# Chunk states of a linear scan: six steps in a row replaced by three doublings with powers of the transition matrix

## The reference, cut to what matters

```python
def step(hc, u_t):
    hc = jnp.einsum('bdr,drs->bds', hc, A) + u_t[:, :, None] * Bv[None]
    y = jnp.einsum('bds,ds->bd', hc, Cv)
    return (hc, y)
_, ys = jax.lax.scan(step, h0, u.transpose(1, 0, 2))
y = ys.transpose(1, 0, 2)
return y @ Wout + b_out + res
```

## Time and profile before

| | us |
|---|---|
| median of three runs | 1939.16 |
| lowest and highest run | 1934.07, 1939.63 |
| the profiled execution | 1942.1 |
| its span in the trace | 1940.4 |
| busy in the span: TensorE matmul / weight load | 1724.4 / 1318.3 |
| busy in the span: DVE / ACT / POOL | 1185.5 / 979.3 / 852.3 |

### The profile page before, as it was taken

The page is one execution under the profiler, slowest core; times in us unless marked ns, Lnnn a source line. Parts: engine busy times, 40 slices in busy tenths (PEclk is TensorE's granted clock), DMA queues, the critical chain, the costliest instruction groups (busy, mean ns, idle before and its releaser), DMA issues.

```text
span 1940.4 us, 25449 instructions
## 1 busy us (share of the span) xinstructions
PE 1724.4 (89%) x8004; PEld 1318.3 (68%) x8004; DVE 1185.5 (61%) x2758; ACT 979.3 (50%) x1906; POOL 852.3 (44%) x866
## 2 busy tenths in 40 slices
PE   6989998779999899999999888889899888888799
PEld 6979997757767677776767655656665555555565
DVE  5542215767677777767686825444356666677765
ACT  3612001656556656565656667666545444445442
POOL 3841201335555545454545453444457666651100
PEclk9989558789999999999999989898899888889999
DMA  6001001087332323233223452221001101002233
GB/s 85 1 2 24 1 1 33 17 198 180 107 93 91 98 85 98 88 98 93 93 88 118 122 149 66 66 86 42 28 12 33 29 23 23 23 31 74 81 109 93
DMA packets 131183, 134.92 MB, mean 70 GB/s; under 512 B 56614, under 2 KB 75306, under 8 KB 131050
## 3 DMA queue, kind: packets, MB, share of 16 engines
q1 hardware_dynamic: 120904, 132.35, 24.5%
q10 hardware_dynamic: 10146, 0.94, 0.6%
HBM read 127.93 MB, written 5.31 MB: 69 GB/s over the span
## 4 chain that ended last, share of the span: by engine, by line
PE 39%; DVE 18%; ACT 12%; issue 7%; POOL 4%; DMA 2%; SPq 1%; DVEq 0%; ACTq 0%; POOLq 0%
PE ypsum L1156 7%; PE flow_G L100 4%; PE flow_G L102 3%; PE flow_G L101 3%; DVE flow_a L1701 2%; DVE flow_a L1707 2%; PE flow_U L100 2%; DVE flow_phi L1485 2%; PE flow_U L101 2%; PE flow_U L102 2%; POOL flow_alo L1790 2%; ACT flow_ahi L1186 1%; ACT xn_tokens L1218 1%; PE flow_side L100 1%; DVE flow_at_rneg L1673 1%
## 5 line engine op out<-in xcount | busy, mean ns | idle before, releaser
L1790 POOL TENSOR_TENSOR flow_alo<-flow_a,flow_ahi 128x512 fp32r<-128x512 f32 x264 | 341.6, 1294 | 339.8 <-ACT flow_ahi L1186 339.3
L100 PE MATMUL flow_G<-xn_hi,flow_hi 128*128 128x512 f32 x520 | 283.9, 546 | 37.6 <-DVE flow_a L1701 22.4
L1701 DVE TENSOR_TENSOR flow_a<-flow_G,flow_mask 128x512 f32<-128x512 f32 x256 | 175.7, 686 | 160.8 <-ACT flow_G L1360 135.4
L1360 ACT ACTIVATE flow_G<-flow_G 128x512 f32<-128x512 f32 x256 | 149.0, 582 | 141.1 <-PE flow_G L102 140.5
L101 PE MATMUL flow_G<-xn_lo,flow_hi 128*128 128x512 f32 x520 | 212.6, 409 | 0.0
L102 PE MATMUL flow_G<-xn_hi,flow_lo 128*128 128x512 f32 x520 | 212.1, 408 | 0.0
L1707 DVE TENSOR_TENSOR flow_a<-flow_U,flow_a 128x512 f32<-128x512 f32 x296 | 204.7, 691 | 9.9
L1186 ACT ACTIVATE flow_ahi<-flow_a 128x512 fp32r<-128x512 f32 x264 | 165.4, 627 | 86.6 <-DVE flow_a L1707 85.5
L1799 POOL TENSOR_TENSOR flow_b<-flow_b,flow_mask 128x512 f32<-128x512 f32 x96 | 126.8, 1327 | 148.5 <-ACT flow_b L1364 77.7
L1799 POOL TENSOR_TENSOR flow_a<-flow_a,flow_mask 128x512 f32<-128x512 f32 x96 | 127.8, 1342 | 105.8 <-ACT flow_a L1364 54.4
L100 PEld LDWEIGHTS flow_G<-xn_hi,flow_hi 128*128 128x128 f32 x520 | 102.2, 197 | 103.9 <-issue 42.2
(11 more groups left out here) (535 smaller groups left out, 3936.3 us busy)
## 6 DMA issues: line engine op xcount, KB each, us to landing
flow_mask<-mask_rows_top SPq DMA_DIRECT2D x512, 128.0 KB, 3.0
flow_mask<-mask_rows_top SPq DMA_DIRECT2D x64, 256.0 KB, 3.2
flow_mask<-mask_rows_zone SPq DMA_DIRECT2D x64, 256.0 KB, 3.2
flow_mask<-mask_rows_steps SPq DMA_DIRECT2D x32, 256.0 KB, 4.0
x<-in_L_attn_x SPq DMA_DIRECT2D x8, 256.0 KB, 5.9
flow_raw<-in_L_ffn_expert_gate_k SPq DMA_DIRECT2D x16, 128.0 KB, 3.6
flow_raw<-in_L_ffn_expert_up_k SPq DMA_DIRECT2D x16, 128.0 KB, 3.6
flow_raw<-in_L_ffn_expert_down_k SPq DMA_DIRECT2D x16, 128.0 KB, 3.9
```

Source lines behind the costliest of these rows:

```text
L100: pe.matmul(out, w_hi, x_hi, start=start, stop=False)
L1360: act.activation(gate, gate, ACT.Silu).then_inc(ev["r_done"], 1)
L1701: dve.tensor_tensor(out, G[at % 2].psum[:, :], weight, ALU.mult).then_inc(ev["t_done"], 1)
L1790: pool.tensor_tensor(alo[i][:, :], acts[i][:, :], ahi[i][:, :].bitcast(F32), ALU.subtract)\
```

## The change

The chunk states are carried by doubling. With P32 the 32nd power that is at hand, and h the states:

1. `one_chunk(i)`: 32 matmuls (4 in each of 8 rounds) with P32, 96 columns (chunks 1 to 6 of 16 sequences); DVE adds the result to chunks 2 to 7.
2. `turned_power(i)`: 32 transposes of P32 into the tile `power`, copied by ACT. `squared(i)`: 32 matmuls with 128 columns, of `power` and P32, give the 64th power, transposed as a stationary operand needs it; ACT copies it to `square`.
3. `two_chunks(i)`: 32 matmuls with the 64th power, 80 columns (chunks 1 to 5); DVE adds to chunks 3 to 7.
4. `four_chunks("half", i)` and `four_chunks("four", i)`: the 128th power as the 64th twice, 2 x 32 matmuls with 48 columns (chunks 1 to 3), 8 in a round; between the two ACT copies to the tile `middle`; behind the second DVE adds to chunks 5 to 7.

`power`, `square` and `middle` lie in `early`, where the pieces of `T0` lie that the near rounds have used. The order on TensorE becomes: 16 near rounds, with a `turned_power` or a `one_chunk` behind each in turn; then `squared` and `two_chunks` in turn, the second two behind the first; then four rounds `half` and four rounds `four`; then the far rounds as before. The 40 state rounds use the same ring of four banks; each waits until the round four before it is evicted, and for what it reads. Far rounds wait for the `four` round of their packs.

```diff
+        self.Hn = self.AT[:, :, :].rearrange("p g m -> p (g m)")[:, 0:PACKS * P].rearrange("p (q n) -> p q n", n=CHUNKS)
+        self.power, self.square = (early[:, 4096 * i:4096 * (i + 1)].rearrange("p (g m) -> p g m", m=P) for i in range(2))
+        self.middle = early[:, 0:PACKS * 48].rearrange("p (g m) -> p g m", m=48)
...
+        def begin(kind, i):
+            n = rounds.number[kind, i]
+            if n >= 4:
+                rounds.wait_evicted(pe, ev, n - 4)
+            return (bank[3], bank[4], bank[5], k.turn)[n % 4]
+
+        def chunk_states(p, first, after):
+            return s.H[:, p, :].rearrange("p (b n) -> p b n", n=CHUNKS)[:, :, first:after]
+
+        def turned_power(i):
+            out = begin("power", i)
+            for q in range(4):
+                last = pe.transpose(out[:, q * P:(q + 1) * P], A[:, 4 * i + q, 0:P], k.ident[:, :])
+            last.then_inc(ev["state_psum"], 1)
+
+        def one_chunk(i):
+            out = begin("one", i)
+            for q in range(4):
+                last = pe.matmul(out[:, q * 96:(q + 1) * 96], A[:, 4 * i + q, 0:P], chunk_states(4 * i + q, 1, 7), start=True, stop=True)
+            last.then_inc(ev["state_psum"], 1)
+
+        def squared(i):
+            rounds.wait_evicted(pe, ev, rounds.number["power", i])
+            out = begin("square", i)
+            for q in range(4):
+                last = pe.matmul(out[:, q * P:(q + 1) * P], s.power[:, 4 * i + q, :], A[:, 4 * i + q, 0:P], start=True, stop=True)
+            last.then_inc(ev["state_psum"], 1)
+
+        def two_chunks(i):
+            rounds.wait_evicted(pe, ev, rounds.number["square", i])
+            rounds.wait_evicted(pe, ev, rounds.number["one", i])
+            out = begin("two", i)
+            for q in range(4):
+                last = pe.matmul(out[:, q * 80:(q + 1) * 80], s.square[:, 4 * i + q, :], chunk_states(4 * i + q, 1, 6), start=True, stop=True)
+            last.then_inc(ev["state_psum"], 1)
+
+        def four_chunks(kind, i):
+            if kind == "half":
+                rounds.wait_evicted(pe, ev, rounds.number["two", 2 * i + 1])
+            else:
+                rounds.wait_evicted(pe, ev, rounds.number["half", i])
+            out = begin(kind, i)
+            for q in range(8):
+                p = 8 * i + q
+                x = chunk_states(p, 1, 4) if kind == "half" else s.middle[:, p, :]
+                last = pe.matmul(out[:, q * 48:(q + 1) * 48], s.square[:, p, :], x, start=True, stop=True)
+            last.then_inc(ev["state_psum"], 1)
...
         def far(r):
             if r == 0:
                 pe.wait_ge(ev["h_zero"], 1)
-                pe.wait_ge(ev["sc_done"], SUBS * (CHUNKS - 2))
                 pe.wait_ge(ev["y_near"], 16)
+            if r % 4 == 0:
+                rounds.wait_evicted(pe, ev, rounds.number["four", r // 4])
...
-        done = 0
-        for n in range(1, CHUNKS - 1):
-            for sub in range(SUBS):
-                if n > 1:
-                    pe.wait_ge(ev["sc_done"], SUBS * (n - 2) + sub + 1)
-                out = (bank[3], bank[4], bank[5], k.turn)[sub]
-                for i in range(8):
-                    p = 8 * sub + i
-                    last = pe.matmul(out[:, i * BATCH:(i + 1) * BATCH], A[:, p, 0:P], s.H[:, p, n:P:CHUNKS],
-                                     start=True, stop=True)
-                last.then_inc(ev["sc_psum"], 1)
-                if (SUBS * (n - 1) + sub) * 16 // 24 >= done:
-                    near(done)
-                    done += 1
-        assert done == 16
+        for r in range(16):
+            near(r)
+            (one_chunk if r % 2 else turned_power)(r // 2)
+        for i in range(10):
+            if i < 8:
+                squared(i)
+            if i >= 2:
+                two_chunks(i - 2)
+        for i in range(4):
+            four_chunks("half", i)
+        for i in range(4):
+            four_chunks("four", i)
         for r in range(16):
             far(r)
```

On ACT a copy of a `power` bank (128x512) stands behind every second near copy, then follow the 8 copies of `square` and the 4 of `middle` (128x384). On DVE the 24 adds (L2434) become 20:

```diff
-        for n in range(1, CHUNKS - 1):
-            for sub in range(SUBS):
-                dve.wait_ge(ev["sc_psum"], SUBS * (n - 1) + sub + 1)
...
+        for kind, i in rounds.order:
+            if kind in rounds.scalar:
+                continue
+            n = rounds.number[kind, i]
+            dve.wait_ge(ev["state_psum"], n + 1)
+            out = (bank[3], bank[4], bank[5], k.turn)[n % 4]
+            first, packs = {"one": (2, 4), "two": (3, 4), "four": (5, 8)}[kind]
+            width = CHUNKS - first
+            h = s.Hn[:, packs * BATCH * i:packs * BATCH * (i + 1), first:CHUNKS]
+            dve.tensor_tensor(h, h, out[:, 0:packs * BATCH * width].rearrange("p (q n) -> p q n", n=width), ALU.add)\
+               .then_inc(ev["state_dve"], 1)
+            if f < PAIRS:
...
```

More of the change, by code:

```diff
@@ L1956, in __init__ @@
                          "shifted stats aggr pool scale_done h_done turned hi lo win_link win_done first bias_done u_psum u_done "
-                         "e_dve e_pool g_turned g_copied ut_turned u2_done v_psum v_done h_zero sc_psum sc_done f_done "
+                         "e_dve e_pool g_turned g_copied ut_turned u2_done v_psum v_done h_zero state_psum state_act state_dve f_done "
                          "t0_in t0_done near_psum y_near y_psum y_done yt_turned yc_act yc_dve", st)
@@ L2199, in near @@
             last.then_inc(ev["near_psum"], 1)
+        rounds = StateRounds()
+        def begin(kind, i):
[39 more added lines that the diff above has]
+            last.then_inc(ev["state_psum"], 1)
         def far(r):
@@ L2241, in _, with __init__, wait_evicted @@
             last.then_inc(ev["yt_turned"], 1)
+class StateRounds:
+    def __init__(self):
+        order = [("one" if r % 2 else "power", r // 2) for r in range(16)]
+        for i in range(10):
+            order += [("square", i)] * (i < 8) + [("two", i - 2)] * (i >= 2)
+        order += [("half", i) for i in range(4)] + [("four", i) for i in range(4)]
+        self.order = order
+        self.number = {key: n for n, key in enumerate(order)}
+        self.scalar = ("power", "square", "half")
+        self.count, n = {}, {"state_act": 0, "state_dve": 0}
+        for key in order:
+            name = "state_act" if key[0] in self.scalar else "state_dve"
+            n[name] += 1
+            self.count[key] = (name, n[name])
+    def wait_evicted(self, pe, ev, n):
+        name, value = self.count[self.order[n]]
+        pe.wait_ge(ev[name], value)
 def finish_y(s, eng, copy, name, parity):
@@ L2313, in _, with state_copy @@
                 .then_inc(ev["u2_done"], 1)
+        rounds = StateRounds()
+        def state_copy(kind, i):
+            n = rounds.number[kind, i]
+            out = (bank[3], bank[4], bank[5], k.turn)[n % 4]
+            act.wait_ge(ev["state_psum"], n + 1)
+            if kind == "half":
+                copy(s.middle[:, 8 * i:8 * i + 8, :], out[:, 0:384].rearrange("p (g m) -> p g m", m=48)).then_inc(ev["state_act"], 1)
+            else:
+                copy((s.power if kind == "power" else s.square)[:, 4 * i:4 * i + 4, :],
+                     out[:, :].rearrange("p (g m) -> p g m", m=P)).then_inc(ev["state_act"], 1)
         for r in range(16):
@@ L2319, in _ @@
                  (bank[0], bank[1], bank[2], k.ypsum)[r % 4][:, :]).then_inc(ev["y_near"], 1)
+            if r % 2 == 0:
+                state_copy("power", r // 2)
+        for i in range(8):
+            state_copy("square", i)
+        for i in range(4):
+            state_copy("half", i)
         finish_y(s, act, copy, "yc_act", 0)
@@ L2428, in _ @@
         dve.wait_ge(ev["v_done"], 8)
-        for n in range(1, CHUNKS - 1):
-            for sub in range(SUBS):
-                dve.wait_ge(ev["sc_psum"], SUBS * (n - 1) + sub + 1)
[L2432 to L2441, removed]
+        rounds = StateRounds()
+        for kind, i in rounds.order:
+            if kind in rounds.scalar:
+                continue
+            n = rounds.number[kind, i]
+            dve.wait_ge(ev["state_psum"], n + 1)
+            out = (bank[3], bank[4], bank[5], k.turn)[n % 4]
+            first, packs = {"one": (2, 4), "two": (3, 4), "four": (5, 8)}[kind]
[4 more added lines that the diff above has]
+            if f < PAIRS:
+                dve.tensor_tensor(s.F[:, 2 * f:2 * f + 2, :, :],
+                                  A[:, 2 * f:2 * f + 2, P:P + CHUNK].unsqueeze(2).to_broadcast([P, 2, PACK, CHUNK]),
+                                  s.mask8[:, :].unsqueeze(1).unsqueeze(3).to_broadcast([P, 2, PACK, CHUNK]), ALU.mult)\
+                   .then_inc(ev["f_done"], 1)
+                f += 1
         for r in range(16):
```

## The result

The changed kernel took 1892.44 us in the median of 4 runs (1891.74 to 1895.07), the kernel before 1939.39 us in 4 runs on the same chip: 46.95 us less, ratio 0.9758 with a 95% interval of 0.9735 to 0.9782. A second set of runs, later, gave 1892.55 against 1941.42 us, ratio 0.9745 (0.9726 to 0.9765). The forecast was 1893.5 us.

A forecast was written before the change was run, and what follows sets the result against it. TensorE bounds the kernel, paying per record for weight loads at a halved clock in the chunk states. 24.1 + 13.8 + 23.8 = 61.7 us against 107.4 saves 45.7: 1893.5 us from the median 1939.16, range 1879 to 1910.

The forecast's parts named there:

- first part: Near rounds, power transposes and `one` rounds: 224 records of 96 to 128 columns at 0.1075 us, 24.1 us.
- second part: `squared` and `two` rounds: 128 records of 128 and 80 columns at 0.1075 us, clock expected to stay, 13.8 us.
- third part: `half` and `four`: 128 records of 48 columns, clock falling 3.4 us after the start, 23.8 us (bounds 13.8 and 27.2).
- stage: Chunk states, from first near or state matmul to first far matmul: 107.4 us before, forecast 61.7 us.
- far rounds: Matmuls after the chunk states: forecast to start at the low clock as before and cost the same 16.4 us.
- saved in the stage: Chunk-state time removed minus time added: 45.7 us, forecast to come off the whole kernel.
- The step with no row behind it: In `half` and `four`: a stream of 48 columns alone, seen in no row, was taken to lose the clock after 3.4 us.
- The waits: In the chunk states: TensorE's waits for ACT, DVE and POOL all hidden; without cover in `squared`/`two`, at most 2 us.
- kept throughout: Rival, chance 0.16: full clock through `half`, `four` and the far matmuls, 58.3 us saved, 1880.9 us.
- Clock lost from the second part on: Rival, chance 0.12: the 80 columns of `two` lose the clock, 32.3 us saved, 1906.9 us.
- the change gives no clock back: Rival, chance 0.08: something other than columns keeps the chunk states' clock low, 8.8 us saved, 1930.4 us.
- The slower rival: Rival, chance 0.03: all 40 state rounds wait for the eviction just ahead, at low clock; 31.2 us slower, 1970 us.

The follow-up runs named there:

- Experiment 1: Kernel before, its six steps and 512 records kept, each state matmul moving 64 columns instead of 16, of which DVE takes 16: 1887.51 us, ratio 0.9717.
- Experiment 3: Changed kernel, order kept, every matmul of one, squared, two, half and four cut to 16 columns, other columns left out: 1911.36 us, ratio 0.9845.
- experiment 4: Changed kernel with 64 columns instead of 48 in the matmuls of half and four: 1884.09 us, ratio 0.9700; in a second set 1878.07 us, ratio 0.9686.
- experiment 5: Changed kernel, every state round waiting for the eviction of the round just ahead instead of four ahead: 1928.02 us, ratio 0.9925 to the kernel before.
- experiments 1 and 2: The second of these: kernel before, 16-column state matmuls reading neighbouring columns of H instead of every eighth, states thus wrong: 1942.11 us, ratio 1.0007.

## Why the prediction was right

**The reading of the bottleneck.** It said that TensorE never waited for DVE in the chain of steps, that a record pays for its weight load and not its columns, and that the granted clock was the larger lever. Experiment 1 bears out the first, the third and half of the second: same records, same chain, four times the columns, 58.3 us. Experiment 3 adds that at full clock narrower matmuls are no cheaper. That it is the weight load which a record pays for stays argued: it fits that TensorE's weight loads fill the stage (106.3 of 107.4 us), but no run made the weight load smaller.

**The terms of the sum.**

| term | forecast, us | measured, us |
|---|---|---|
| first part, 224 records | 24.1 | 25.0 |
| second part, 128 records | 13.8 | 14.3 |
| third part, 128 records | 23.8 | 23.0 |
| stage | 61.7 | 62.3 |
| far rounds | 16.4 | 16.6 |
| saved in the stage | 45.7 | 45.1 |

The price of a record was low, by a misread view. The 93 and 447 records of the earlier trace rows do not all start in their stretch; the view counts each record that lies in it even partly, and at 1.00 a record lasts about 0.27 us while the next start follows after 0.11. The order of time in the same stretch has 24 records in 2.64 us, 0.110 each:

```profile
178.73 1.94 PE L2175 MATMUL ssm_bank<-ssm_turned,ssm_mix 128*128 128x112 f32 x16
180.50 0.60 PE L2163 MATMUL ssm_bank<-ident,ssm_early 128*128 128x128 f32 x4
180.94 0.60 PE L2163 MATMUL turn<-ident,ssm_early 128*128 128x128 f32 x4
181.37 1.94 PE L2175 MATMUL ssm_bank<-ssm_turned,ssm_mix 128*128 128x112 f32 x16
```

Measured are 25.01 us for 224 records, 0.1116 us each, which makes the first two parts 1.4 us longer than forecast. The third part came out 0.8 us shorter, because the clock went 4.6 us into it instead of the 3.4 us taken over from before. With the right prices the forecast's own path would have given about 63.6 us for the stage (an estimate: 352 records at 0.1116, then 30 in 3.4 us, then 98 at 0.213), so a part of the agreement of 61.7 with 62.3 is two errors that cancel.

The step with no row behind it, that 48 columns alone lose the clock, came out as taken, and experiment 4 shows that this was not for another reason of the third part. It was the closest call, and partly luck: the reason given was that nothing in the part is wide, yet 64 columns, in the same place and order, keep the clock.

That 1892.44 us lies 1.1 us from the forecast is chance in part as well: in the two traces the code behind the barrier, which was forecast to stay as long, differs by 3.6 us.

**The waits.** All were hidden. DVE's add was 0.553 us where 0.6 was taken between 0.52 and 1.17. POOL's last `T0` piece began at 201.9 us, well ahead of near round 15.

**The rivals.** The clock was not kept throughout; the 58.3 us saved that this rival gave are nearly what experiment 4 has (107.4 + 16.4 before, 53.6 + 13.9 with 64 columns: 56.4). Clock lost from the second part on is what experiment 5 made happen, by gaps and not by the 80 columns. That the change gives no clock back fell with its own trace (1.00 in the first two parts) and with experiments 1 and 2. The slower rival's mechanism costs 35.5 us and not the 77 that it was priced at, since the near rounds cover it in the first part and the clock holds there; with it the kernel is still faster than before, if by under 1% (0.9925). So the price of that rival was too high, and this mechanism alone does not end on the slower side.

**What the doubling itself is worth.** Both orders at full clock: 53.6 us (experiment 4) against 58.3 (experiment 1), 4.7 us. Of these, 32 fewer records are 3.6 at 0.1116 us, and the wait of `far(0)` for the last near copy, which the new order no longer has, is 0.9. So about a tenth of the gain comes from doubling and its order, the rest from the clock that its wider matmuls hold.

## What to carry to other kernels

Look at the granted clock of a stretch before its dependency chain: a TensorE that is busy throughout at 0.50 takes about twice as long as at 1.00 (0.213 us against 0.1116 for a record here), and matmuls that move few columns behind a full 128x128 weight load are a place where it happens. Columns are then free, or better than free, as far as 128 here: from 16 to 128 columns a record took the same 0.11 us at full clock, with 256 it took 0.215. So widen the moving operand with data that is at hand, throw away the results that are not needed, and check in the trace that the next stretch also starts at full clock. Keep evictions several rounds ahead, because gaps cost their own time and can take the clock as well (17 us each in experiment 5).

## What the runs showed of the hardware that was not expected

**Computing columns that are then thrown away makes a stage faster.** In the same place and order, 48 columns alone were at 1.00 for 4.6 us and then at 0.50; 64 columns alone stayed at 1.00 for the 14.3 us that they lasted.

**Identical code behind the barrier took 1605.5 to 1616.0 us** in nine traces. A part of the spread lies in the projection, where TensorE has pauses and the clock changes level several times. From the barrier to the first gate matmul of the experts it took 74.8 us in the kernel before, 76.5 in both traces of the changed kernel, and 70.9 and 71.0 in those of the 64-column version. Another part lies behind that matmul: from there to the end of the span it took 1539.8 us in the kernel before and 1534.4 and 1534.6 in the changed one. So the 3.6 us between the two are 5.3 us less in the experts and what follows, and 1.7 us more in the projection. The stretch from 30 to 45 us behind the barrier, first in the changed kernel, then in the second trace of the 64-column version:

```profile
309.99:324.99 15.00, 13.59 (x90) 12.65 (x89) 11.46 (x68) 8.78 (x28) 4.17 (x10) 0.73 0.09 20
```

```profile
298.47:313.47 15.00, 12.47 (x111) 11.98 (x109) 14.20 (x89) 11.44 (x37) 3.83 (x11) 1.00 0.12 28
```

The same code gets 111 records done at 1.00 and 90 at 0.73. Two traces of the same version agree within 0.3 us behind the barrier, so in the traces the spread goes with the version; the untraced runs of the 64-column version, near 1884 to 1887 us, show that this is not all of it. Whether it is the moment at which the projection starts that decides its clock was not tried. For a comparison of two versions it means that a difference of 5 us, and up to 10 in these traces, can come from code that neither of them touches.
